# A graph network's running sums of a source stage as one scan over rows laid out by feature

## What is computed

```
h = relu(layernorm(x));  x = x + A(A h)             # A h: sum over edges of weight * h[src] into row dst, twice
h = relu(layernorm(x));  x = x + norm_gcn(h @ W) + b          # each edge scaled by 1/sqrt(deg) at both ends
h = relu(layernorm(x));  x = x + relu((h + sum h[src]) @ W1.T + b1) @ W2.T + b2
h = relu(layernorm(x));  x = x + update(h, segment_sum(message(h[src], h[dst], edge_attr), dst))
```

## Time and profile before

| | |
|---|---|
| median of 3 runs | 4681.54 us (4678.89 to 4682.18) |
| the profiled execution's own time | 4679.67 us |
| its span in the trace | 4677.9 us |
| DVE / PE / POOL / ACT busy, share of the span | 64% / 76% / 72% / 43% |
| stage 0's steps in the span | about 2200 to 2814 us |
| stage 1's steps in the span | about 2916 to 3513 us |

### The profile page before, as it was taken

The page is one execution under the profiler, slowest core; times in us unless marked ns, Lnnn a source line. Parts: engine busy times, 40 slices in busy tenths (PEclk is TensorE's granted clock), DMA queues, the critical chain, the costliest instruction groups (busy, mean ns, idle before and its releaser), DMA issues. The chain is left out here.

```text
span 4677.9 us, 61963 instructions
## 1 busy us (share of the span) xinstructions
PE 3541.6 (76%) x18706; PEld 2847.4 (61%) x18706; DVE 3005.6 (64%) x7259; ACT 2010.3 (43%) x5132; POOL 3351.3 (72%) x2841
## 2 busy tenths in 40 slices
PE   5756565656628999996777777888855998898894
PEld 3444444444418999995655655667645776776773
DVE  5544444444416565554998995999966877777771
ACT  3434343434311111112565564666632665555552
POOL 5777777777757888887666753766756677777764
PEclk8767676767655555556999998999977999999996
DMA  6232323232224444442443432445443323333220
GB/s 219 44 57 45 57 45 57 45 57 45 41 41 66 72 68 72 68 61 38 137 130 108 140 114 78 159 158 182 155 161 105 119 86 112 102 96 114 84 78 21
DMA packets 324110, 426.13 MB, mean 91 GB/s; under 512 B 207631, under 2 KB 225525, under 8 KB 323380
## 3 DMA queue, kind: packets, MB, share of 16 engines
q1 hardware_dynamic: 147908, 335.87, 20.6%
q0 software_dynamic: 176000, 87.72, 15.5%
HBM read 245.53 MB, written 212.59 MB: 98 GB/s over the span
## 5 line engine op out<-in xcount | busy, mean ns | idle before, releaser
L921 POOL DMA_INDIRECT ga<-table,isl x784 | 813.4, 1038 | 247.7 <-issue 230.2
L950 POOL DMA_INDIRECT hop<-acc,osl x392 | 629.6, 1606 | 218.7 <-issue 108.6
L985 POOL DMA_INDIRECT xu<-acc,osl x392 | 619.5, 1580 | 141.7 <-issue 102.5
L1178 PE MATMUL tp<-us,wide 128*128 128x64 f32 x1568 | 340.3, 421 | 338.6 <-DVE us L1914 338.6
L1048 POOL DMA_INDIRECT out_x<-acc,osl x392 | 432.0, 1102 | 184.1 <-issue 118.6
L1178 PEld LDWEIGHTS tp<-us,wide 128*128 128x128 f32 x1568 | 335.8, 332 | 345.0 <-issue 344.9
L921 POOL DMA_INDIRECT ga<-xu,isl x392 | 419.7, 1071 | 121.5 <-issue 113.4
L1230 PE MATMUL tp<-us,wide 128*128 128x64 f32 x1568 | 416.8, 422 | 103.1 <-DVE wide L2108 103.1
L921 POOL DMA_INDIRECT ga<-in_x,isl x392 | 398.5, 1017 | 119.5 <-issue 95.0
L1193 PE MATMUL tp<-xw,cc 128*128 128x394 f32 x784 | 401.1, 607 | 108.6 <-ACT found L1515 94.4
L1230 PEld LDWEIGHTS tp<-us,wide 128*128 128x128 f32 x1568 | 380.0, 332 | 107.7 <-issue 79.9
(11 more groups left out here) (369 smaller groups left out, 8566.1 us busy)
## 6 DMA issues: line engine op xcount, KB each, us to landing
wide<-xu SPq DMA_DIRECT2D x84, 448.0 KB, 4.7
zx<-key_rows SPq DMA_DIRECT2D x28, 896.0 KB, 4.5
out_x<-wide SPq DMA_DIRECT2D x56, 448.0 KB, 5.0
table<-acc SPq DMA_DIRECT2D x56, 448.0 KB, 2.8
xf<-xs SPq DMA_DIRECT2D x56, 448.0 KB, 3.6
wide<-table SPq DMA_DIRECT2D x56, 448.0 KB
xu<-in_x SPq DMA_DIRECT2D x25, 1000.0 KB, 5.6
hop<-zeros SPq DMA_DIRECT2D x1, 12544.0 KB, 37.6
```

The source lines that it names most:

```text
L921: nc.gpsimd.indirect_dma_start(o[:, g, :], None, table, bass.IndirectOffsetOnAxis(idx[:, g:g + 1], 0)).then_inc(s, 16)
L950: nc.gpsimd.indirect_dma_start(hop, bass.IndirectOffsetOnAxis(osl[b][:, g:g + 1], 0), acc[b][:, g, :], None, bounds_check=hop_max, oob_is_ ...
L985: nc.gpsimd.indirect_dma_start(xu, bass.IndirectOffsetOnAxis(osl[b][:, g:g + 1], 0), acc[b][:, g, :], None, bounds_check=all_max, oob_is_e ...
L1178: t = nc.tensor.matmul(o[:, g * D:g * D + D], equal[b][:, c, (g % 2) * P:(g % 2) * P + P], us[b][:, c, :], start=n == 0, stop=n == 1)
```

## The change

The sums of a unit become one `tensor_tensor_scan` over 960 numbers in each partition. For that the rows h of a unit, and the loaded rows hin, are laid out by feature: 64 runs (one for each feature) of G + 1 = 15 numbers, of which the first is a border column and the other 14 are the unit's columns. WS = 15 * 64 = 960. The border column of h takes the last sums of the unit before. Its factor is 0, so the scan starts anew at each feature with that carried value. ScalarE spreads the factors `same` over the 64 features into the same layout (`source_factor`, two copies a pass), and copies the sums back to row layout in acc (`source_sums`, two copies a pass). `source_normal` writes h, and the sums with the gathered rows read hin, with a step of 15 numbers (60 bytes) from feature to feature.

```diff
-        ms1, hs2 = dram("ms1", [P, T * D]), dram("hs2", [P, T * D])
+        ms1, hs2 = dram("ms1", [P, U * WS]), dram("hs2", [P, U * WS])
...
+        def led(t):
+            return t.rearrange("p (d g) -> p g d", g=G + 1)
+
+        def by_row_of(t):
+            return led(t)[:, 1:G + 1, :]
...
+            def source_factor(k, i, b):
+                n = k * STEPS + i
+                if n:
+                    act.wait_ge(*summed.at(n - 1, ("a", b)))
+                else:
+                    nc.scalar.copy(led(factor[b])[:, 0, :], zeros[:, 0:D])
+                shared = same[:, ecol(i, b):ecol(i, b) + G].unsqueeze(2).broadcast_to([P, G, D])
+                led_factor.raise_by(nc.scalar.copy(by_row_of(factor[b]), shared), ("f", b))
+
+            def source_sums(k, i, b, first):
+                f = sp_[k]
+                act.wait_ge(*summed.at(k * STEPS + i, ("a", b)))
+                if not first:
+                    act.wait_ge(f.stored[b], 16 * i)
+                elif k:
+                    act.wait_ge(sp_[0].stored[b], 16 * STEPS)
+                f.acc_ready.raise_by(nc.scalar.copy(full(acc[b]), by_row_of(sums_f[b])), ("a", b))
...
                 dense_std(j, "l1", 0)                                # ScalarE's list
                 if k is not None:
+                    for b in B2K:
+                        source_factor(k, i, b)
                     ln_squares(sp_[k], i, [0], "l", source_c[k], "v" if k else None)
...
                 dense_std(j, "l2", 1)
+                if k is not None:
+                    source_sums(k, i, 0, first)
                 dense_copy(j, "h1", 0)
                 dense_copy(j, "h2", 1)
                 dense_square(j, "l2", 0)
+                if k is not None:
+                    source_sums(k, i, 1, first)
...
             def source_sum(own, i, b):
-                f.ga_free.raise_by(V.tensor_tensor(full(us[b]), full(hin[b]), full(ga[b]), ALU.add), ("g", b))
+                f.ga_free.raise_by(V.tensor_tensor(full(us[b]), by_row_of(hin_f[b][:, :]), full(ga[b]), ALU.add), ("g", b))
...
             def source_normal(own, k, i, b, first):
+                if first and b == 0:
+                    V.memset(led(h_f[b][:, :])[:, 0, :], 0.0)
+                else:
+                    own.wait(summed.at(n, ("a", 0)) if b else summed.at(n - 1, ("a", 1)))
+                    V.tensor_copy(led(h_f[b][:, :])[:, 0, :], led(sums_f[1 - b])[:, G, :])
                 own.wait(marks[k, b])
-                if not first:
-                    dve.wait_ge(*f.acc_ready.at(i - 1, ("a", b)))
-                    dve.wait_ge(f.kept[b], 16 * 2 * i)
-                f.state_ready.raise_by(V.scalar_tensor_tensor(full(h[b]), full(source_c[k][b]), 0.0, stat(b, 3), ALU.max, ALU.mult),
-                                       ("x", b))
+                f.state_ready.raise_by(V.scalar_tensor_tensor(by_row_of(h_f[b][:, :]), full(source_c[k][b]), 0.0, stat(b, 3),
+                                                              ALU.max, ALU.mult), ("x", b))
...
-            def source_run(own, k, i, b, first):
-                running(own, i, b, lambda g: acc[b][:, g, :], prev, 0, lambda g: h[b][:, g, :], same, ecol(i, b),
-                        ready, range(G), final=lambda ins: f.acc_ready.raise_by(ins, ("a", b)))
+            def source_run(own, k, i, b):
+                f, n = sp_[k], k * STEPS + i
+                own.wait(f.state_ready.at(i, ("x", b)))
+                dve.wait_ge(*led_factor.at(n, ("f", b)))
+                if n:
+                    dve.wait_ge(*(f.acc_ready.at(i - 1, ("a", b)) if i else sp_[0].acc_ready.at(STEPS - 1, ("a", b))))
+                summed.raise_by(V.tensor_tensor_scan(sums_f[b], factor[b], h_f[b][:, :], 0.0, ALU.mult, ALU.add), ("a", b))
```

More of the change, by code:

```diff
@@ L21 @@
 W = G * D
+WS = (G + 1) * D
 HB = G // 2
@@ L238, in gnn @@
         unit = [P, G, D]
-        hin, xw, h, vt, ga = (pair(n, unit) for n in ("hin", "xw", "h", "vt", "ga"))
+        xw, vt, ga = (pair(n, unit) for n in ("xw", "vt", "ga"))
+        hin_f, h_f = (pair(n, [P, WS]) for n in ("hin", "h"))
+        hin, h = ([t[:, 0:W].rearrange("p (g d) -> p g d", d=D) for t in ts] for ts in (hin_f, h_f))
         xf = sb("xf", [P, 4, G, D])
         xin, first_sq = [xf[:, b] for b in range(2)], [xf[:, 2 + b] for b in range(2)]
-        zx = sb("zx", [P, 4, G, D])
+        zx_all = sb("zx", [P, 2 * W + 2 * WS])
+        zx = zx_all[:, 0:4 * W].rearrange("p (k g d) -> p k g d", k=4, g=G)
+        factor = [zx_all[:, 2 * W + b * WS:2 * W + (b + 1) * WS] for b in range(2)]
         zz, x3 = [zx[:, b] for b in range(2)], [zx[:, 2 + b] for b in range(2)]
@@ L716, in dense_store, with unit_rows @@
                     sp.dma_start(node_rows(out, l, q), full(lane_o[q])).then_inc(s_dense[q], 16)
+            def unit_rows(t, c):
+                return t[:, c // G * WS:c // G * WS + WS]
             def source_load(i, b):
-                for t, s in ((xin, xs1), (hin, ms1)):
-                    sp.dma_start(flat(t[b]), s[:, bass.ds(ecol(i, b) * D, W)]).then_inc(sp_[1].load[b], 16)
+                sp.dma_start(flat(xin[b]), xs1[:, ecol(i, b) * D:ecol(i, b) * D + W]).then_inc(sp_[1].load[b], 16)
+                sp.dma_start(hin_f[b][:, :], unit_rows(ms1, ecol(i, b))).then_inc(sp_[1].load[b], 16)
             def source_state(k, i, b):
@@ L759, in t_load @@
                 at = bass.ds(tcol(i, b) * D, W)
-                for t, s in ((xin, xs2), (hin, hs2), (a3, rows(tables[0]))):
-                    sp.dma_start(flat(t[b]), s[:, at]).then_inc(tt.load[b], 16)
+                sp.dma_start(flat(xin[b]), xs2[:, at]).then_inc(tt.load[b], 16)
+                sp.dma_start(hin_f[b][:, :], unit_rows(hs2, tcol(i, b))).then_inc(tt.load[b], 16)
+                sp.dma_start(flat(a3[b]), rows(tables[0])[:, at]).then_inc(tt.load[b], 16)
                 after.wait_ge(*tt.gx_free.at(i - 1, ("g", b)))
@@ L784, in first_rest @@
                     after.wait_ge(tt.load[b], 16 * 4)
-                    for t, s in ((hin, hs2), (xin, xs2)):
-                        sp.dma_start(flat(t[b]), s[:, bass.ds(tcol(0, b) * D, W)]).then_inc(tt.load[b], 16)
+                    sp.dma_start(hin_f[b][:, :], unit_rows(hs2, tcol(0, b))).then_inc(tt.load[b], 16)
+                    sp.dma_start(flat(xin[b]), xs2[:, bass.ds(tcol(0, b) * D, W)]).then_inc(tt.load[b], 16)
             def one_pass(k, i, first, j, l, between=None):
@@ L2323, in one_pass @@
                 if k is not None:
-                    source_run(own, k, i, 0, first)
+                    source_run(own, k, i, 0)
                 dense_add(j, "x2", 1)
@@ L2333, in one_pass @@
                 if k is not None:
-                    source_run(own, k, i, 1, first)
+                    source_run(own, k, i, 1)
                 dense_add(j, "x2", 0)
@@ L2413, in last_pass @@
                         own.wait((tt.got_a[b], 16 * G * (j + 1)))
-                        tt.rows.raise_by(V.tensor_tensor(full(us[b]), full(hin[b]), full(ga[b]), ALU.add), ("us", b))
+                        tt.rows.raise_by(V.tensor_tensor(full(us[b]), by_row_of(hin_f[b][:, :]), full(ga[b]), ALU.add), ("us", b))
                     for b in B2K:
```

28 lines of the change are left out of this document (12 added, 16 removed).

## The result

| kernel | runs | median us | range |
|---|---|---|---|
| before | 4 | 4681.86 | 4678.89 to 4683.56 |
| after | 4 | 4941.56 | 4937.26 to 4948.86 |

The ratio is 1.0557, with a 95% interval from 1.0541 to 1.0573: 260 us slower. The profiled execution of the changed kernel took 4938.73 us (span 4937.0).

A forecast was written before the change was run, and what follows sets the result against it. DVE is busiest, with PE and ACT close behind and little slack at the sums. 14 x 0.8 + 11 x 1.2 - 5 = +19.4 us on 4679.67, plus 1.9 to the median: 4701 us; range 4658 to 4800.

The forecast's parts named there:

- Strides: 60-byte steps in h, hin, factor and sum copies: likeliest no cost, at most +0.87 us per DVE operation, +0.61 on ACT.
- the second rival: Strided access costs on DVE and ACT: 4748 us with one engine, 4794 with both, at most 4818; chance 0.27.
- I take +1.2 as the value, since those gaps become no shorter: Stage 1 pass: +1.65 us, or +0.45 if PE's 14 transposes lose their slow pace; +1.2 taken.
- 0.8 forecast, 0.6 to 1.6: Stage 0 pass: +0.8 us taken, from the copy of sums 1 (0.6) and possible slow PE passes (about another 1.0).
- x2 1: DVE sum after `source_run` 0, needing PE's product h1 1: starts +1.0 us later in stage 1, as factor copies delay ACT.
- Removed and added on DVE: Source passes: chain of 4.36 us replaced by scan of 2.1 and border copy of 0.13; DVE's list 4.2 us shorter a pass.
- Copy of sums 0 hidden: ACT's copy of sums 0 lies in the 2.48 us ACT waits for PE's transposes: costs nothing, otherwise 0.86 us.
- copy of sums 1 at +0.5: ACT, between square of l2 0 and relu h2 1: takes 0.86 us less a 0.26 wait; +0.5 us in stage 1.
- The end of stage 1: -5 us: No dense work beside: last two chains become scans and copies, -3.4 us; one chain before them, -2.1; together -5 us.
- The t stage: No term in the sum; if strided access costs, its two reads add up to 24 us of DVE, partly hidden.
- The first rival: DVE's saving comes through: 4662 us if ACT has room for factor copies, 4564 if PE and ACT keep pace; chance 0.14.
- the third: Nothing measurable: PE keeps full pace in all passes, giving back what the copies cost; about 4682 us, chance 0.04.

The follow-up runs named there:

- the probe: Kernel before with 28 extra DVE and ACT operations of 128x768 numbers at steps of 1 to 64 numbers ahead of its first loads: 4722.95 us.
- the copies alone: Kernel before with two extra contiguous ACT copies in each source pass at the place of the factor copies, which nothing reads: 4748.02 us, ratio 1.0141.
- the wait filled: Kernel before with two extra ACT copies a pass and one spare PE product ahead of back product h3 1 in stage 1: 4696.39 us, ratio 1.0029.

## Why the prediction was wrong

The direction was right and so was the reason for it: DVE's shorter list does not show, because PE's products end beside it. The size, +19 instead of +260 us, was wrong by two steps, and the kernel with all accesses contiguous, at 4797 us, divides the 240 us between them: 144 and 96. This division holds for taking the steps away first. The parts overlap, since spare products alone gave back 120 us of the changed kernel, more than the 96 that are left without steps.

**Strides: "the likeliest to me is nothing, because each number is already taken at about 1 ns".** This step failed. The price is 0.61 us for a DVE operation, inside the bound of 0.87, and 0.80 us for an ACT copy (1.72 and 1.73 us against 0.92 and 0.93 contiguous), above the bound of 0.61. That bound was also worked out unevenly: the slope of 0.74 ns times 896 numbers, as for DVE, gives 0.66. The bound took the slope as the most that a step can add; on ACT it adds more. In sum steps cost 144 us, where the second rival had 117 up to its top of 4818; the 144 also hold what the lower clock made of the longer copies. Its chance of 0.27 was too low: a row that does not exist says nothing for "nothing". What the prediction cites against it from the Trainium skill ("Advanced Engine Details and Errata", section Memory Cachelines), a penalty for a new 16-byte line at each access, agrees with the probe, 0.96 against 1.46 us at a step of 60 bytes.

**"I take +1.2 as the value, since those gaps become no shorter".** This step failed too. It looked at PE's existing slow stretch, the transposes, and asked only whether its 1.2 us would come back. It did not ask what the copies do to PE ahead of the back product h3 1. In the kernel before PE waits there for 0.3 us at most; the copies make it 0.9 us in stage 0 and 1.7 in stage 1 when they are contiguous, and 2.2 to 2.4 and 3.0 with steps. Behind this wait PE does 2 x 1.67 + 1.72 = 5.1 us of work on the path, and in the changed kernel it took up to 3.09 + 3.09 + 3.30 = 9.5. With the copies alone in stage 1 a delay of 1.4 us a pass became 5.4. Where this stretch kept its pace, the sum was good: a pass of 45.54 us in stage 0 with all contiguous is +1.2 on the 44.3 of before (0.8 forecast, 0.6 to 1.6), and +1.4 in stage 1 with the wait filled stands against the +1.0 for "x2 1" (that run has no border copy). As an estimate from the pass lengths of the kernel with all contiguous, eight passes of stage 0 at 5.7 us more than the short ones, and in stage 1 493.6 us instead of ten times its shortest pass of 46.8, make about 70 of the 96 us; the rest was not assigned.

**Removed and added on DVE.** The scan took 2150 ns (2.1 forecast), the border copy 197 ns (0.13). DVE is busy 2.2 us less in a stage 0 pass instead of 4.2; two state writes at +0.61 account for 1.2 of the difference.

**Copy of sums 0 hidden, copy of sums 1 at +0.5.** The second one ahead of relu h2 1 was mis-sized: it takes 1.7 us, makes PE wait 3.19 us (1.58 or 2.72 before) and DVE 1.6 (0.4 before) for the root of l2 0, and the back product h2 1 behind it is slow (1.50 us for six products that take 0.83), as it was before in some passes only the earlier trace rows. The share of this place alone was not measured. **A wait that the prediction has not at all** is DVE's 2.2 us in a stage 0 pass for the root of l1 1, which stands behind the factor copies on ACT. DVE waits again afterwards, 2.29 us for the back product h3 1, so what the first wait costs by itself is not shown. With the factor copies moved away, 101 us are left.

**The end of stage 1: -5 us.** Measured +4.4: the three passes there took 116.0 instead of 111.7 us. What of it is whose was not taken apart. **The t stage**, priced at nothing in the sum, cost 14.3 us: 26 reads at +0.62 are 16, so next to nothing of it is hidden.

**The first rival** (faster) and **the third** (nothing) did not happen. The forecast's sign that copies near 1.6 us or `source_normal` near 2 would mean the second rival was the right one to look at.

## What to carry to other kernels

A layout that suits one instruction is paid for by every neighbour that reads or writes across it: count each such access, and measure its step in a few operations ahead of the kernel before building on it. An engine that is idle for a third of the time may have no room at one place; put work for it where it waits for the chain, not where the chain waits for it. When a wait on TensorE gets longer, price the work behind it at both clock levels: a delay of 1.4 us cost 5.4, and a spare product in the wait took 4.0 of it back, while in the kernel before, where the filled stretch was off the path, spare products gave nothing.

## What the runs showed of the hardware

A step of 2 numbers (8 bytes) is free for float32 on DVE (0.96 us for 768 numbers) and nearly so on ACT (0.88 against 0.83), and one of 4 (16 bytes) costs as much as any tested up to 64: 1.45 to 1.53 us on DVE and 1.48 to 1.56 on ACT, but for the one DVE write of 2.87. The scan over 960 numbers takes 2.15 us. One kernel can run its passes in two lengths, 45.5 and 51.1 us, with all instructions and the busy times of DVE and ACT alike, and with the same wait of 0.9 us ahead of the products that took 1.67 or 3.09 us. And the kernel before took 4682 us in most runs and 5806 to 5898 in others, where changes don't even keep their sign (0.968 against 1.021 for the factor copies moved).
